# Unused products in TensorE's idle stretches at both ends, and a gate product moved ahead of a power, in a gated layer kernel

## What is computed

```python
x = x + tanh(g_xattn) * xattn(ctx, ctx, layernorm(x), ssm_kernel, D)   # causal convolution by head
x = x + tanh(g_ffn) * ffn(layernorm(x), conv_w, Wq, Wk, Wv, Wg, router_w, Wout)

# xattn: 32 heads of dimension 8, L = 512
kv  = einsum('bhil,bhjl->bijhl', k, v)
out = causal_conv(kv, ssm_kernel) + kv * D
out = einsum('bijhl,bhil->bjhl', out, layernorm(x))

# ffn: 16 heads, head value width 32, sequences of 256 rows, x of shape (16, 256, 512)
x = silu(x_prev * conv_w[:, 0] + x * conv_w[:, 1])
q, k, v, g = silu(x @ Wq), x @ Wk, x @ Wv, x @ Wg         # q and k rotated
...                                                       # two-way router, masked scores
o = einsum('bhlm,bhmd->bhld', qk, v)
o = (o - mean(o)) / sqrt(var(o) + 1e-5)                   # per head, width 32
out = (silu(g) * o) @ Wout
```

## Time and profile before

| | |
|---|---|
| median of 3 runs | 910.64 us (909.43 to 911.76) |
| profiled execution, its own time | 909.48 us |
| its span, first to last instruction | 907.7 us |
| PE busy | 863.7 us (95%) |
| DVE, POOL, ACT busy | 712.7 (79%), 725.8 (80%), 434.6 us (48%) |
| chain that ended last | PE 88%, issue 4%, DVE 3%, POOL 2% |
| mean granted TensorE clock | 0.984 |

### The profile page before, as it was taken

How to read it: one execution, slowest core, us unless ns; L and a number is a source line. 1 busy time by engine, 2 the same in 40 slices (tenths; PEclk the granted TensorE clock), 3 DMA queues, 4 the chain that set the end, 5 groups by cost and what they waited for, 6 DMA issues and landing times.

```text
span 907.7 us, 17997 instructions
## 1 busy us (share of the span) xinstructions
PE 863.7 (95%) x6592; PEld 732.3 (81%) x6592; DVE 712.7 (79%) x1521; ACT 434.6 (48%) x941; POOL 725.8 (80%) x611
## 2 busy tenths in 40 slices
PE   4889999999999999999999999999999999999974
PEld 3768888888888888888888888888888888888762
DVE  4788877787887778788777878877787897778741
ACT  3655455444545544454554544455454545544320
POOL 6779888899888889988888998888899888886331
PEclk9999999999999999999999999999999999999995
DMA  9310222211222221122222112222211222210000
GB/s 268 106 53 1 65 65 65 64 32 36 63 65 65 65 64 35 34 63 66 64 65 65 38 30 63 65 65 65 65 40 28 63 65 65 65 48 12 4 15 18
DMA packets 26679, 51.83 MB, mean 57 GB/s; under 512 B 3232, under 2 KB 4640, under 8 KB 26592
## 3 DMA queue, kind: packets, MB, share of 16 engines
q1 hardware_dynamic: 22320, 46.19, 19.1%
q10 hardware_dynamic: 4272, 4.48, 1.5%
HBM read 42.12 MB, written 8.55 MB: 56 GB/s over the span
## 4 chain that ended last, share of the span: by engine, by line
PE 88%; issue 4%; DVE 3%; POOL 2%; ACT 1%; DMA 1%; POOLq 0%; SPq 0%; ACTq 0%; DVEq 0%
PE bank L335 38%; PE bank L306 24%; PE bank L284 9%; PE bank L293 6%; PE bank L387 4%; PE bank L372 4%; PE bank L319 2%; PE bank L322 1%; DVE z_terms L844 1%; DMA z_terms<-in_L_xattn_D 1%; PE bank L445 0%; POOL kv L695 0%; POOL rstd L710 0%; POOLq L67 0%; POOL o_rstd L710 0%
## 5 line engine op out<-in xcount | busy, mean ns | idle before, releaser
L306 PE MATMUL bank<-kv_pair,toep 128*128 128x512 f32 x960 | 244.9, 401 | 1.3 <-DVE z_terms L835 1.3
L704 POOL TENSOR_TENSOR kv_pair<-kv,kv_pair 128x576 fp32r<-128x576 f32 x126 | 179.0, 1432 | 51.3 <-ACT kv_pair L537 51.3
L306 PEld LDWEIGHTS bank<-kv_pair,toep 128*128 128x128 f32 x960 | 175.0, 189 | 41.7 <-DVE z_terms L835 6.7
L695 POOL TENSOR_TENSOR kv<-kx 128x512 f32<-128x512 f32 x128 | 173.0, 1351 | 5.6 <-DMA kx<-in_ctx 3.9
L710 POOL TENSOR_TENSOR o_rstd<-o_ve,minus_half 128x16 f32<-128x16 f32 x32 | 93.1, 2908 | 83.5 <-DVE o_ve L921 83.5
L537 ACT ACTIVATE kv_pair<-kv 128x576 fp32r<-128x576 f32 x128 | 87.8, 687 | 106.8 <-POOL kv L698 105.9
L335 PE MATMUL bank<-w_all_high,yT_high 128*128 128x512 f32 (+2 forms) x512 | 120.9, 358 | 0.8 <-DVE gated L952 0.8
L844 DVE TENSOR_TENSOR z_terms<-z_terms 128x512 f32<-128x512 f32 (+1 forms) x96 | 116.6, 1240 | 0.0
L335 PE MATMUL bank<-w_all_low,yT_high 128*128 128x512 f32 (+2 forms) x512 | 112.6, 342 | 0.0
L1017 DVE SCALAR_TENSOR_TENSOR out_sb<-bank,gates,x 128x512 f32<-128x512 f32 x32 | 24.0, 751 | 106.0 <-PE bank L335 106.0
L335 PE MATMUL bank<-w_all_high,yT_low 128*128 128x512 f32 (+2 forms) x512 | 105.9, 339 | 0.0
(11 more groups left out here) (110 smaller groups left out, 1595.9 us busy)
## 6 DMA issues: line engine op xcount, KB each, us to landing
toep<-taps_dram SPq DMA_DIRECT2D x31, 512.0 KB, 7.1
kx<-in_ctx SPq DMA_DIRECT2D x32, 384.0 KB, 7.4
x_in<-in_x SPq DMA_DIRECT2D x32, 256.0 KB
out_x<-out_sb SPq DMA_DIRECT2D x32, 256.0 KB
wv_t<-in_L_ffn_Wv ACTq DMA_DIRECT2D x1, 1024.0 KB, 8.0
w_g<-in_L_ffn_Wg ACTq DMA_DIRECT2D x1, 1024.0 KB, 6.9
w_out<-in_L_ffn_Wout ACTq DMA_DIRECT2D x1, 1024.0 KB, 10.5
w_qk<-in_L_ffn_Wq ACTq DMA_DIRECT2D x1, 512.0 KB, 4.5
```

What stands on the lines that cost most here:

```text
L306: ins = nc.tensor.matmul(bank[lc % 2][:, :], toep[:, 1 - p, a, (lc - mc) * P:(lc - mc + 1) * P], kv_p[b][:, 1 - p, mc, 0:FULL], start=(mc ...
L695: eng.tensor_tensor(view(kv[:, c % 2, 0:FULL], [[ROW, NROT], [1, ROW]]), view(kx[:, p, c, 0:ROW], [[0, NROT], [1, ROW]]), view(kx[:, p, c, ...
L704: eng.tensor_tensor(kv_p[1][:, p, c, :], kv[:, c % 2, :], kv_p[0][:, p, c, :].bitcast(F32), ALU.subtract).then_inc(kv_ready[c], 1)
```

## The change

A semaphore `z_zeroed` is added, and DVE's list begins by setting `z` to zero. TensorE's list begins with a wait for it and nine calls of a 128x512 product of `z` with itself into bank 6; the results are not used. In the last step two such calls into bank 0 stand ahead of `attention_output`, and five behind the transposes of `oT`; `z` holds there what ACT wrote for the last tile. On DVE, the product with the gate moves to right behind `o_ve`, reading bank 4, and the product with `o_rstd` comes second, in place on `gated`. The semaphore that frees bank 4 (`o_normed`, now `o_gated`) is raised by the first of the two.

```diff
@@ TensorE
+            def keep_busy(ps, n):
+
+                for _ in range(n):
+                    nc.tensor.matmul(ps[:, :], z[:, 0:P], z[:, :], start=True, stop=True)
+
+            eng.wait_ge(z_zeroed, 1)
+            keep_busy(bank[6], 9)
             eng.wait_ge(s_consts, 16)
...
+                if h == LAST:
+                    keep_busy(bank[0], 2)
                 if tail:
                     attention_output()
...
                     transpose4(bank[4], lambda c: oT[:, c, :], o_ps)
+                if h == LAST:
+                    keep_busy(bank[0], 5)
...
-                        eng.wait_ge(o_normed, h)
+                        eng.wait_ge(o_gated, h)
                     project(bank[4], yT_p, w_all_p, V0, DV, v_ps, y_low, h + 1)
@@ VectorE
+            eng.memset(z[:, :], 0.0).then_inc(z_zeroed, 1)
...
                                              op0=ALU.mult, op1=ALU.add).then_inc(o_ve_ready, 1)
+                    eng.wait_ge(gate_ready, h)
+                    if can_wait(h - 1):
+                        eng.wait_ge(gatedT_ps, h - 1)
+                    eng.tensor_tensor(gated[:, :], bank[4][:, :], gate_sb[:, :], ALU.mult).then_inc(o_gated, 1)
                 if pre and h != -1:
                     norm_x(t, p, h)
...
                     eng.wait_ge(o_rstd_ready, h)
-                    if can_wait(h - 1):
-                        eng.wait_ge(gatedT_ps, h - 1)
+                    eng.wait_ge(o_gated, h)
                     eng.tensor_tensor(gated[:, :].rearrange("p (a n) -> p a n", n=HDV),
-                                      bank[4][:, :].rearrange("p (a n) -> p a n", n=HDV),
-                                      view(o_rstd[:, 0:1], [[1, RH], [0, HDV]]), ALU.mult).then_inc(o_normed, 1)
-                    eng.wait_ge(o_normed, h)
-                    eng.wait_ge(gate_ready, h)
-                    eng.tensor_tensor(gated[:, :], gated[:, :], gate_sb[:, :], ALU.mult).then_inc(gated_ready, 1)
+                                      gated[:, :].rearrange("p (a n) -> p a n", n=HDV),
+                                      view(o_rstd[:, 0:1], [[1, RH], [0, HDV]]), ALU.mult).then_inc(gated_ready, 1)
```

More of the change, by code:

```diff
@@ L183, in flamingo_gated_layer @@
             sem(n) for n in ("qk_low", "logit_low", "g_low", "v_low", "wout_low"))
+        z_zeroed = sem("z_zeroed")
         conv_last_ps, last_copied, last_added = sem("conv_last_ps"), sem("last_copied"), sem("last_added")
@@ L210, in flamingo_gated_layer @@
          qke_ready, bn1_done, mv1_done, ve1_ready, nmr1_ready, qn_ready, x2_ready, bn2_done, mv2_done,
-         ve2_ready, nmr2_ready, z_ready, o_summed, o_ve_ready, o_normed, gated_ready) = (
+         ve2_ready, nmr2_ready, z_ready, o_summed, o_ve_ready, o_gated, gated_ready) = (
             sem(n) for n in ("mul_last", "y_conv", "out_ready", "ad_ready", "u_ready", "th1_ready", "rth1_ready",
@@ L214, in flamingo_gated_layer @@
                              "nmr1_ready", "qn_ready", "x2_ready", "bn2_done", "mv2_done", "ve2_ready",
-                             "nmr2_ready", "z_ready", "o_summed", "o_ve_ready", "o_normed", "gated_ready"))
+                             "nmr2_ready", "z_ready", "o_summed", "o_ve_ready", "o_gated", "gated_ready"))
         FIRST, LAST = -2, NH
```

## The result

941.32 us, median of 6 runs (939.67 to 944.18), against 910.39 us before in the same session (908.37 to 911.76, 6 runs); ratio 1.0349, interval [1.0331, 1.0367]. Forecast was 904.4.

A forecast was written before the change was run, and what follows sets the result against it. TensorE was taken to bound the middle (busy 398.54 of 400 us), leaving gains at the ends. Last step 4.9, bank 4 0.4 and ramp 0.9 sum to 6.2 us, from 910.64 to 904.4; range 902.8 to 907.6.

The forecast's parts named there:

- The step that failed: Middle steps: the moved gate product costs nothing, as work behind gets its 0.69 us back; at most 0.69.
- Case 5: Middle steps: moved product delays `u` or `mul_last` beyond their spare, 0.2 us a step, 910.6 us in all; chance 0.05.
- Last step, 4.9: Last step: fillers hold TensorE's clock and one product leaves the chain, together 4.9 us less.
- case 3: Last step: clock falls between the fillers or after the second, 1.1 to 2.5 us less gain; chance 0.18.
- Price of a filler call, 0.85 us: Fillers on TensorE: one 512-column call takes four passes, 0.85 us at full clock, 1.71 at half.
- Bank 4, 0.4: TensorE's wait for bank 4: freed some 4 us earlier, gaining 0.4 of at most 0.8 us.
- Ramp, 0.9: Ramp: nine filler calls raise the clock, `first_rest(3)` and what follows come 0.7 to 1.1 us earlier, taken as 0.9.
- case 2: Ramp: no gain, as the clock falls in idle time or zero products don't count, 905.3 us; chance 0.17.
- The rule on transposes: TensorE's clock: the skill says transposes don't count like matmuls; the prediction read the trace at 30 to 32 us against it.

The follow-up runs named there:

- 3: Changed kernel, fillers kept, gate product still first of the two but put back behind DVE's first sum of halves: 905.5 us, 0.9954 of the kernel before.
- 5: Changed kernel plus two unused one-column powers on POOL ahead of its first rotation product in each step with a tail: 904.06 us, 0.9942 of the kernel before.
- 7: Kernel before plus four unused 128x16 operations on DVE right behind `o_ve`: 943.42 us, 1.0371 of the kernel before.
- run 4: Changed kernel with the gate product right behind `o_ve` in the last step only, behind DVE's first sum elsewhere: 905.86 us, 0.9952 of the kernel before.
- run 2: Kernel before plus all fillers and the zeroing of z, gate products in old order: 908.36 us, 0.998 of the kernel before.
- 8: Kernel before plus only the last step's two fillers (2 and 5 calls), gate products in old order: 907.37 us, 0.9977 of the kernel before.
- 10: As run 4, without the ramp's fillers and with 6 calls instead of 5 in the last step's second filler: 904.85 us, 0.9952 of the kernel before.
- 11: Changed kernel with one extra one-column POOL power a step, no ramp fillers, 2 and 6 last-step calls: 917.58 us, 1.0088 of the kernel before.
- 12: Changed kernel with two extra POOL powers a step, no ramp fillers, 2 and 6 last-step calls: 904.83 us, 0.9939 of the kernel before.
- 9: Kernel before plus only the zeroing of z and the ramp's nine filler calls: 910.6 us, 1.0013 of the kernel before.
- 1: Changed kernel without any filler or the zeroing of z, so only the gate product moved: 943.98 us, 1.0369 of the kernel before.
- 6: Kernel before plus one unused 128x16 operation on DVE right behind `o_ve`: 923.85 us, 1.0157 of the kernel before.

## Why the prediction was wrong, step by step

- **The step that failed**: "The two products that follow `add_halves` become one, so what stands behind gets its 0.69 back. ... So a middle step costs nothing; if the spare were gone, it would cost up to 0.69." `add_halves` itself stands ahead of that point and was moved by 0.6 us past the start of POOL's rotation product, and DVE's operations that take both tensors from SBUF don't run beside POOL's products. The prediction took every duration as fixed, and counted only semaphore waits, not which of the two engines starts first. Nor did it price the one wait that came to count, that of TensorE for the last sum of halves, where it had 0.5 us to spare and the sum came 1.46 us later. The loss was 1.27 us a step in 29 steps, where the prediction had nothing and 0.69 as the most. The place alone decides (3 against the changed kernel); the order of starts decides (5, where more POOL work takes the loss away; 7, where 0.43 us of DVE work brings it without the change). The trace of the kernel before had shown it: the first rotation product lasted 2.18 us in the middle but 1.27 in the step before the last, and DVE's `gated` product 1.06 against 0.69 in the last step, where POOL is idle.
- The Trainium skill, SBUF — State Buffer, "SBUF: two separate sides", says of the read and write ports that DVE and GpSimd share: an exclusive lock, "whichever ... starts first gets the pair for the whole instruction; the other fully blocks", with a DVE operation of two SBUF inputs among those that take it, against a GpSimd operation that reads SBUF. For POOL's products the traces agree: the second starter's record ends 1.09 and 1.14 us behind the first one's end, which is about the length of its own work (1.2 to 1.3 us when nothing is in its way), in either order. For POOL's powers they don't: in run 5 the first sum starts inside a power, lasts 1.21 us as it does alone, and the `o_rstd` product, started at 450.75 inside a power that runs to 451.24, lasts 0.68. So the measured rule is narrower than the page's.
- **Case 5** (the moved product costs the middle) had the right place and 0.05 for a chance, but named the wrong wait: TensorE's wait for `u` was 1.8 us in 3 times, 1.5 in 2 before; the 0.8 us of spare held. The price, 0.2 us a step, was a guess from the spare and not from a row.
- **Last step, 4.9**: right in mechanism and size when the clock holds through the projection (4.95 in run 4; 4.2 without the product in run 2). In the changed kernel and in the profiles of 3 and 8 it fell ahead of or in the projection, which is case 3 (1.1 to 2.5 less; 3.37 instead of 4.9). It did so in 3 of the 6 profiles with five calls and in none of the 3 with six (10, 11, 12): a chance of 0.18 was too low, as far as six profiles tell. Why it falls in some of these executions and not in others stays open.
- **Price of a filler call, 0.85 us**: ten instructions in 4.46 us, so about 0.43 apart, 0.86 a call. Right. The ramp's nine ended at 12.5, within 11 to 12.8.
- **Bank 4, 0.4**: the wait is gone from the changed kernel; without meaning beside the rest.
- **Ramp, 0.9**: `first_rest(3)` did start 0.77 us earlier, within the 0.7 to 1.1 forecast, though the first transposes themselves came 0.39 us later. But 0.49 us of the lead went to the same exclusion (1.24 instead of 0.75), and the first z came 0.21 us earlier. Alone, the ramp's fillers gave no gain (9), and in four of six profiles the clock fell again at 15.2 to 16.0 us, which is what case 2 had as one of its reasons, with a chance of 0.17. Whether they delay the first loads stays open: the first transposes stood at 13.5 to 15.4 us in the eight profiles without them, and at 13.9 to 15.5 in the six with them.
- **The rule on transposes**: the earlier trace rows start too late to show where the clock fell. It fell at 28.41 us, in the middle of work, and came back at 31.83 (columns as the earlier trace rows):

```profile
28.00:28.40 0.40, 0.40 (x6) 0.40 (x5) 0.40 (x2) 0.40 (x2) 0.40 (x1) 1.00 0.00 0
28.40:28.80 0.40, 0.40 (x4) 0.30 (x2) 0.40 (x2) 0.40 (x1) 0.40 (x2) 0.52 0.00 0
```

From the fall on, TensorE did transposes alone, and full clock followed, so the reading in the prediction holds. But ahead of the fall TensorE was busy without a gap, with 128x4 products (24.85 to 27.89) and the first 0.65 us of these transposes. An idle gap is thus not the only thing that goes ahead of a fall, as the cases of the prediction took it. Between the fillers of the last step the clock held in every profile; that stretch is too short to speak for or against the rule.
- **A fall that no filler covers**: the step before the last also has one, at 864.7 us in the kernel before (row 865:866 in the earlier trace rows). From the scores before it to the last scores it is 21.0 to 21.7 us in the three profiles without this fall (the changed kernel, 5 and 12) and 22.1 to 23.6 in the eleven with it. The prediction has no term for it. The three without it all have the early gate product, but so have 1 and 11, in which it fell.

## What to carry to other kernels

Where DVE and POOL both work on SBUF for most of a step, a move in one list is priced by who starts first at each meeting of the two, not only by semaphores: line up their start times relative to one event and look for pairs that change places. The pairs that count here are a DVE operation with both tensors in SBUF and a product on POOL. A record on DVE or POOL that is longer than the same operation takes elsewhere can be a wait in disguise. And where a move is only wanted in the last step, make it there alone.

## What the runs showed of the hardware that was not expected

- The exclusion is steep: 0.1 us of extra DVE work a step cost 14 us in all (6), 0.43 us cost 34 (7), while two extra powers on POOL a step won 37 (5 against the changed kernel).
- With 0.1 us of delay the steps alternate, 27.5 and 26.4 us, as each order sets up the other.
- It is not the same for every operation of POOL. DVE sums and products with both inputs in SBUF that start inside a power keep their 1.21 and 0.68 us (5). A one-column power takes 0.55 us by itself, 0.80 when it starts inside a short DVE product with both inputs in SBUF, and 1.44 when it starts inside the first sum (5).
- A DVE product with one input from a bank keeps its 0.62 to 0.69 us beside POOL's products, in all profiles.
